# Last row tile of an attention and dense layer: its final product cut into 384 and 128 columns in place of 256 and 256

## The chip, the core and the metric

The kernel runs on one core of a Trainium2 chip. The metric is the time of one execution on the device in microseconds (us); three runs of the kernel before took 237.77, 237.84 and 237.99 us, median 237.84 us. TensorE multiplies matrices, VectorE (DVE) and ScalarE (ACT) work elementwise, GpSimd (POOL) does elementwise work and issues some transfers, and SyncE (SP) issues most transfers between device memory and on-chip memory.

## The reference, cut to what matters

The input `x` is 2048 rows of 512 columns. Each row is normalized, and two branches are added to it:

```python
xn  = layernorm(x)
q   = xn @ Wq.T + bq                      # only one head in four is used: 8 heads of 128
s   = elu(q) + 1
num = s @ M                               # per head, 128 x 128
den = s . z + 1e-6
att = repeat(num / den, 4) @ Wo.T         # back to 512 columns
ffn = xn @ (w.astype(float32) * w_scale) + b
out = x + att + ffn                       # 2048 x 512, float32
```

## The kernel before, in words

The 2048 rows are 16 tiles of 128 rows, called t = 0 to 15 (`T` = 16). The weights `Wo` are first summed over the four repeats and multiplied with `M` into one matrix `P` per head (8 heads, `G` = 8, each 128 x 512), so that the attention branch of a tile is one product: sum over the 8 heads of (128 rows x 128) by (128 x 512).

Every float32 product is made in three passes over operands split in two parts, a rounded high part and the rest, both in the format `F32R`. The function `three_passes` (L875 to L878) issues them: high by high (L876), then L877 and L878 with one low part each. In the rows of the trace the operand named `P_hi` or `P_lo` is the one that streams through TensorE (its columns set the width of the instruction), and `aT_hi` or `aT_lo` is the one loaded ahead into the array as weights, 128 x 128, by an instruction LDWEIGHTS (engine PEld in the trace).

TensorE is given its work in a written order: a start-up part, then for t = 7 to 15 the two q products, the dense product and the attention product of the tile eight before (`LAG` = 8), then the attention products of the remaining tiles 8 to 14 (`product_attn`, L951), and at last tile 15 (L1059 to L1068). A short transpose of the row means, `spread_mean` (L886), stands between the products in the loop.

Tile 15 differs from the others. Its 512 output columns are made in two pieces, c = 0 and c = 1, of 256 columns each, into two accumulators in different banks: `attn_ps[1]` and `q_ps[0]` (`last_attn_ps`, L106). For each piece TensorE runs over all 8 heads with three passes, 24 matmuls, and announces the piece on the semaphore `attn_filled`. VectorE waits for it and adds the accumulator onto the piece of `x` (L866 to L871, the instruction of L870), then announces `attn_added`. SyncE waits for that and issues the write of the piece to device memory (L300 to L303, the transfer of L303), and at the end waits for all writes (L304). While TensorE works on the second piece, the first is added and written.

The waits of TensorE for tile 15 stand only in the first piece: for the operands of tile 15 (`aT_lo_ready`) and for the accumulator to be free (`attn_added`).

Of the kernel before, what the change touches and what calls it, by code (L numbers as in the profile page):

```python
# [18 lines left out]
def retrieval_and_dense(nc, x_d, xT_d, x_pair_d, xT_pair_d, WqT_d, bq_d, WoT_d, MT_d, z_d, w_d, wscale_d, b_d, out_d):  # L19


    P = 128
    T, _, HID = x_d.shape
    _, G, D = MT_d.shape
    R, K, _, E = WqT_d.shape
    HALF = E // 2
    GH = G // 2
# [12 lines left out]
    with ExitStack() as ctx:  # L40
# [3 lines left out]
        def bank(name):  # L44
            return ctx.enter_context(nc.psum_tensor(name, [P, 512], F32))
# [50 lines left out]
        q_ps = [bank(f"q{i}_ps") for i in range(4)]  # L96
        dense_ps = bank("dense_ps")
        attn_ps = [bank("attn0_ps"), bank("attn1_ps")]
        mean_ps = bank("mean_ps")

        def q_bank(t, h):
            if t < LEAD and t % 3 == 1:
                return attn_ps[h]
            return q_ps[2 * (t % 3 == 2 if t < LEAD else t % 2) + h]

        def last_attn_ps(c):  # L106
            return [attn_ps[(T - 1) % 2], q_ps[0]][c][:, 0:HID // 2]

        x_in = [sem(f"x_in{t}") for t in range(T)]
        xT_in = [sem(f"xT_in{t}") for t in range(T)]  # L110
# [59 lines left out]
        def halves(h):  # L170
            return slice(h * HALF, (h + 1) * HALF)
# [13 lines left out]
        def place(t):  # L185
            return {T - 6: 2, T - 5: 3, T - 2: 2, T - 1: 3}.get(t, int(t >= 2 and t % 2 == 0))

        def aT_place(t):
            return [aT[:],
                    MT[:].rearrange("p g d -> p (g d)").rearrange("p (i e) -> p i e", i=4),  # L190
                    xT[:, 0:2].rearrange("p t k r -> p (t k r)").rearrange("p (i e) -> p i e", i=4),
                    xT[:, 2:4].rearrange("p t k r -> p (t k r)").rearrange("p (i e) -> p i e", i=4)][place(t)]

        def place_free(t):
            if t in (T - 6, T - 5):
                return xT_lo_ready, t + 5 + (t == T - 5)
            return aT_lo_ready, 2 * t - (6 if t >= T - 4 else 2)
# [13 lines left out]
        def groups_by_sync(t):  # L211
            return 4 if t < FIRST_SHARED else 3 if t == FIRST_SHARED else 2
# [4 lines left out]
        @block.sync  # L217
        def _(sp):
            def load_x(t):
                sp.dma_start(x[:, t, :], x_d[t]).then_inc(x_in[t], 16)  # L220

            def load_xT(t):
                if t >= XRING:
                    sp.wait_ge(xT_lo_ready, t - XRING + 2)
                sp.dma_start(xT[:, t % XRING, :, :].rearrange("p k r -> p (k r)"), xT_d[t]).then_inc(xT_in[t], 16)

            def load_wq_half(k, h):
                sp.dma_start(WqT_raw[:, k, halves(h)], WqT_d[0, k][:, halves(h)]).then_inc(wq_half_in[2 * k + h], 16)

            def load_wo(j):  # L230
                sp.dma_start(Wo_sum[:, j * GJ:(j + 1) * GJ, :].rearrange("p g c -> p (g c)"), WoT_d[0, j]
                             ).then_inc(wo_in[j], 16)

            def spread_blocks(t):
                sp.wait_ge(a_turned, t + 1)
                if t == 1:
                    sp.wait_ge(aT_lo_ready, 2)
                elif t == 2:
                    sp.wait_ge(P_filled, G)
                elif t >= 3:  # L240
                    sp.wait_ge(*place_free(t))
                for i in range(groups_by_sync(t)):
                    for j in range(4):
                        sp.dma_start(aT_place(t)[j * 32:(j + 1) * 32, i, :],
                                     sbuf_s[i * 32:(i + 1) * 32, t % SRING, j * E // 4:(j + 1) * E // 4]
                                     ).then_inc(aT_in[place(t)], 16)

            def store(t):
                sp.wait_ge(attn_added, t + 1)
                sp.dma_start(out_d[t], x[:, t, :]).then_inc(stored, 16)  # L250

            load_xT(0)
            load_wq_half(0, 1)
            load_wq_half(1, 0)
            load_wq_half(1, 1)
            load_wq_half(2, 0)
            load_wq_half(2, 1)
            load_wq_half(3, 0)
            load_wq_half(3, 1)
            load_x(2)  # L260
            load_xT(2)
            load_x(0)
            load_x(1)
            sp.dma_start(w_words, w_d).then_inc(w_in, 16)
            sp.dma_start(wd_raw, wscale_d).then_inc(wscale_in, 16)
            load_x(3)
            load_xT(3)
            sp.dma_start(bq_b[:], bq_d.unsqueeze(0).to_broadcast([P, E])).then_inc(bq_in, 16)
            load_wo(0)
            load_x(4)  # L270
            load_xT(4)
            load_wo(1)
            load_x(5)
            load_xT(5)
            sp.dma_start(z_b[:], z_d.unsqueeze(0).to_broadcast([P, E])).then_inc(z_in, 16)
            sp.dma_start(x[:, 6:8, :].rearrange("p t n -> p (t n)"), x_pair_d).then_inc(x_in[6], 16)
            sp.wait_ge(xT_lo_ready, 7 - XRING + 2)
            sp.dma_start(xT[:, 2:4, :, :].rearrange("p t k r -> p (t k r)"), xT_pair_d).then_inc(xT_in[6], 16)
            sp.dma_start(MT[:], MT_d).then_inc(M_in, 16)
            spread_blocks(0)  # L280
            for t in range(FIRST_LENT, LEAD + 4):
                sp.wait_ge(P_filled, t - FIRST_LENT + 1)
                load_x(t)
                load_xT(t)
            spread_blocks(1)
            for t in range(LEAD, T):
                if t + 4 < T:
                    sp.wait_ge(P_filled, t + 4 - FIRST_LENT + 1)
                    load_x(t + 4)
                    load_xT(t + 4)  # L290
                spread_blocks(t - BEHIND - 2)
                if t - LAG >= 1:
                    store(t - LAG - 1)
            for t in range(T - BEHIND - 2, T):
                spread_blocks(t)
                if T - BEHIND - 2 < t < T - 2:
                    store(t - BEHIND - 2)
            for t in range(T - 2 * BEHIND - 1, T - 1):
                store(t)
            for c in range(2):  # L300
                cols = slice(c * HID // 2, (c + 1) * HID // 2)
                sp.wait_ge(attn_added, T + c)
                sp.dma_start(out_d[T - 1][:, cols], x[:, T - 1, cols]).then_inc(stored, 16)  # L303
            sp.wait_ge(stored, 16 * (T + 1))  # L304
# [301 lines left out]
        def _(dve):  # L606
# [257 lines left out]
                    turn_blocks(T - 1)  # L864
                add_attn(t)
            for c in range(2):  # L866
                cols = slice(c * HID // 2, (c + 1) * HID // 2)
                dve.wait_ge(attn_filled, T + c)
                dve.wait_ge(b_added[T - 1], 16)
                nc.vector.tensor_tensor(x[:, T - 1, cols], last_attn_ps(c), x[:, T - 1, cols], ALU.add  # L870
                                        ).then_inc(attn_added, 1)  # L871

        @block.tensor
        def _(pe):
            def three_passes(out, x_hi, x_lo, w_hi, w_lo, start, stop):  # L875
                nc.tensor.matmul(out, x_hi, w_hi, start=start, stop=False)  # L876
                nc.tensor.matmul(out, x_hi, w_lo, start=False, stop=False)  # L877
                return nc.tensor.matmul(out, x_lo, w_hi, start=False, stop=stop)  # L878
# [178 lines left out]
            for t in range(T - LAG, T - 1):  # L1057
                product_attn(t)
            for c in range(2):  # L1059
                cols = slice(c * HID // 2, (c + 1) * HID // 2)  # L1060
                for g in range(G):
                    if c == 0 and g % GH == 0:
                        pe.wait_ge(aT_lo_ready, 2 * (T - 1) + g // GH + 1)
                    if c == 0 and g == 0:
                        pe.wait_ge(attn_added, T - 2)
                    last = three_passes(last_attn_ps(c), aT_hi[:, (T - 1) % 2, g, :], aT_lo[:, (T - 1) % 2, g, :],
                                        P_hi[:, g, cols], P_lo[:, g, cols], g == 0, g == G - 1)
                last.then_inc(attn_filled, 1)  # L1068
# [35 lines left out]
```

## Time and profile before

| what | value |
|---|---|
| median of three runs | 237.84 us |
| the profiled execution, its own time | 237.95 us |
| span in the profile, first to last instruction | 236.1 us |
| TensorE matmuls busy | 232.5 us, 98% of the span, 1037 instructions |
| weight loads (PEld) busy | 188.4 us, 80% |
| VectorE busy | 174.0 us, 74% |
| ScalarE busy | 125.2 us, 53% |
| GpSimd busy | 107.4 us, 45% |
| mean granted TensorE clock | 1.000 |

The span runs from the first to the last instruction; the time of the execution is 1.85 us more. Matmuls are pipelined: the trace draws each one longer than the distance to the next, so the pace of TensorE is read from the starts of successive instructions and not from their durations. Weight loads run beside the matmuls on a row of their own. "Landing" of a transfer is the time from its issue until its data has arrived.

### The profile page before, as it was taken

The numbers are of one execution on the slowest core, as the hardware profiler recorded it, in microseconds if no ns is written. First come the engines' busy times: TensorE is split into PE (matmuls) and PEld (weight loads), VectorE is DVE, ScalarE is ACT, GpSimd is POOL, SyncE is SP. The second block draws the span as 40 slices with busy tenths as digits, with TensorE's granted clock in tenths as the row PEclk, the third lists the DMA queues.
The fourth block names the chain that finished last, engine by engine and source line by source line (L and its number), as shares of the span: only waits on it lengthen the run. The fifth ranks groups of instructions, "written<-read, shape, count | busy, mean of one in ns | idle before, by whom it ended". The sixth has DMA issues, their size and how long they took to land.

```text
span 236.1 us, 3421 instructions
## 1 busy us (share of the span) xinstructions
PE 232.5 (98%) x1037; PEld 188.4 (80%) x1037; DVE 174.0 (74%) x275; ACT 125.2 (53%) x285; POOL 107.4 (45%) x117
## 2 busy tenths in 40 slices
PE   8999999999999999999999999999999999999995
PEld 3688788888888788888888888888888888888895
DVE  2989999897589987997858859585667879362511
ACT  4845358687298386585547253654637445630300
POOL 1029437856932356558350442524045598480000
PEclk9999999999999999999999999999999999999999
DMA  6999999999590144471727272431134456879521
GB/s 227 389 412 414 356 250 254 224 212 218 133 278 17 41 95 130 96 180 48 175 89 178 72 196 77 91 104 39 52 94 97 136 135 159 191 189 182 193 98 44
DMA packets 24081, 38.76 MB, mean 164 GB/s; under 512 B 5440, under 2 KB 13248, under 8 KB 22912
## 3 DMA queue, kind: packets, MB, share of 16 engines
q1 hardware_dynamic: 18816, 26.10, 33.7%
q0 software_dynamic: 3808, 11.14, 24.5%
q10 hardware_dynamic: 1440, 1.31, 1.9%
q8 instruction: 8, 0.13, 0.2%
q14 instruction: 9, 0.07, 0.1%
HBM read 25.95 MB, written 4.19 MB: 128 GB/s over the span
## 4 chain that ended last, share of the span: by engine, by line
PE 98%; DVE 0%; issue 0%
PE attn_ps L876 14%; PE attn_ps L878 14%; PE attn_ps L877 13%; PE q_ps L876 10%; PE q_ps L878 10%; PE q_ps L877 10%; PE dense_ps L876 6%; PE dense_ps L878 6%; PE dense_ps L877 6%; PE dense_ps L967 2%; PE q_ps L916 1%; PE q_ps L904 1%; PE q_ps L911 1%; PE attn_ps L916 1%; PE attn_ps L904 1%; PE attn_ps L911 1%
## 5 line engine op out<-in xcount | busy, mean ns | idle before, releaser
L489 ACT ACTIVATE s<-s,rden 128x128 f32<-128x128 f32 x128 | 39.2, 390 | 39.3 <-DVE rden L707 37.6
L341 POOL TENSOR_TENSOR e_and_sz<-s,z_b 128x512 f32<-128x512 f32 x32 | 41.7, 1340 | 39.6 <-DVE den L703 39.6
L876 PE MATMUL attn_ps<-P_hi,aT_hi 128*128 128x512 f32 (+1 forms) x136 | 53.0, 389 | 0.0
L878 PE MATMUL attn_ps<-P_hi,aT_lo 128*128 128x512 f32 (+1 forms) x136 | 52.2, 384 | 0.0
L877 PE MATMUL attn_ps<-P_lo,aT_hi 128*128 128x512 f32 (+1 forms) x136 | 52.1, 383 | 0.0
L876 PE MATMUL q_ps<-WqT_hi,xT_hi 128*128 128x512 f32 x104 | 40.7, 391 | 0.0
L878 PE MATMUL q_ps<-WqT_hi,xT_lo 128*128 128x512 f32 x104 | 40.5, 389 | 0.0
L877 PE MATMUL q_ps<-WqT_lo,xT_hi 128*128 128x512 f32 x104 | 40.5, 389 | 0.0
L691 DVE SCALAR_TENSOR_TENSOR q_ps<-q_ps,rstd,bq_b 128x512 f32<-128x512 f32 x28 | 21.0, 752 | 17.6 <-PE q_ps L878 17.6
L876 PEld LDWEIGHTS attn_ps<-P_hi,aT_hi 128*128 128x128 f32 x136 | 25.6, 188 | 6.1 <-issue 0.6
L878 PEld LDWEIGHTS attn_ps<-P_hi,aT_lo 128*128 128x128 f32 x136 | 25.6, 188 | 5.2
L877 PEld LDWEIGHTS attn_ps<-P_lo,aT_hi 128*128 128x128 f32 x136 | 25.6, 188 | 4.7
L316 POOL TENSOR_TENSOR xT<-xT,mean_b 128x512 f32<-128x512 f32 x13 | 18.9, 1454 | 22.9 <-ACT mean_b L430 22.9
L468 ACT ACTIVATE e_and_sz<-q_ps 128x512 f32<-128x512 f32 x28 | 16.6, 594 | 18.1 <-DVE q_ps L691 17.7
L876 PE MATMUL dense_ps<-wd_hi,xT_hi 128*128 128x512 f32 x64 | 25.3, 395 | 0.0
L878 PE MATMUL dense_ps<-wd_hi,xT_lo 128*128 128x512 f32 x64 | 25.0, 390 | 0.0
L877 PE MATMUL dense_ps<-wd_lo,xT_hi 128*128 128x512 f32 x64 | 24.9, 389 | 0.0
L716 DVE STREAM_TRANSPOSE s<-s 128x1024 f32<-128x1024 f32 x16 | 19.7, 1229 | 4.6 <-ACT s L489 4.6
L876 PEld LDWEIGHTS q_ps<-WqT_hi,xT_hi 128*128 128x128 f32 x104 | 19.5, 188 | 4.4 <-DVE xT_lo L650 0.3
L703 DVE TENSOR_REDUCE den<-e_and_sz 128x8 f32<-128x1032 f32 x16 | 19.4, 1214 | 4.8 <-POOL e_and_sz L341 4.8
L878 PEld LDWEIGHTS q_ps<-WqT_hi,xT_lo 128*128 128x128 f32 x104 | 19.5, 188 | 4.1
L877 PEld LDWEIGHTS q_ps<-WqT_lo,xT_hi 128*128 128x128 f32 x104 | 19.5, 188 | 4.0
(96 smaller groups left out, 356.1 us busy)
## 6 DMA issues: line engine op xcount, KB each, us to landing
x<-in_WoT POOLq DMA_DIRECT2D x6, 1024.0 KB, 11.0
x<-in_b POOLq DMA_DIRECT2D x16, 256.0 KB, 4.4
out<-x SPq DMA_DIRECT2D x15, 256.0 KB, 2.4
x<-in_x SPq DMA_DIRECT2D x14, 256.0 KB, 3.6
xT<-in_xT SPq DMA_DIRECT2D x13, 256.0 KB, 3.8
aT<-s SPq DMA_DIRECT2D x104, 32.0 KB, 2.3
MT<-s SPq DMA_DIRECT2D x72, 32.0 KB, 1.9
x<-in_WoT SPq DMA_DIRECT2D x2, 1024.0 KB, 13.3
```

Of the source, the lines that this page charges most:

```text
L316: nc.gpsimd.tensor_tensor(xT[:, t % XRING, :, :], xT[:, t % XRING, :, :], mean_b[:, t % 2, :].unsqueeze(1).to_broadcast([P, K, P]), ALU.su ...
L341: nc.gpsimd.tensor_tensor(sz_eps[:, :, h * D // 2:(h + 1) * D // 2].rearrange("p g (j c) -> p j g c", j=2), by_quarter(sbuf_s[:, t % SRING ...
L468: nc.scalar.activation(e, q_bank(t, h)[:], ACT.Relu, scale=-1.0).then_inc(qneg_ready, 1)
L489: last = nc.scalar.activation(a_g, a_g, ACT.Copy, scale=rden[:, t % 2, g:g + 1])
L691: nc.vector.scalar_tensor_tensor(q_bank(t, h)[:], q_bank(t, h)[:], rstd[:, t:t + 1], bq_b[:, halves(h)], ALU.mult, ALU.add).then_inc(q_bia ...
L703: nc.vector.reduce_sum(den[:, t % 2, :], sz_eps, AX.X).then_inc(den_ready, 1)
L716: nc.vector.transpose(sbuf_s[:, t % SRING, :], sbuf_s[:, t % SRING, :]).then_inc(a_turned, 1)
L876: nc.tensor.matmul(out, x_hi, w_hi, start=start, stop=False)
L877: nc.tensor.matmul(out, x_hi, w_lo, start=False, stop=False)
L878: return nc.tensor.matmul(out, x_lo, w_hi, start=False, stop=stop)
L904: nc.tensor.matmul(q_bank(t, h)[:], xT_hi[:, t, k, :], WqT_hi[:, k, halves(h)], start=k == 0, stop=False)
L911: nc.tensor.matmul(q_bank(t, h)[:], xT_lo[:, t, k, :], WqT_hi[:, k, halves(h)], start=False, stop=False)
```

## The change

The two pieces of tile 15 become 384 columns (`HID - P`) and 128 columns (`P`). The number of instructions, their order, the accumulators, the semaphores and their counts stay. The new helper `last_columns` gives the columns of a piece to SyncE, VectorE and TensorE.

```diff
+        def last_columns(c):
+            return [slice(0, HID - P), slice(HID - P, HID)][c]
+
         def last_attn_ps(c):
-            return [attn_ps[(T - 1) % 2], q_ps[0]][c][:, 0:HID // 2]
+            return [attn_ps[(T - 1) % 2], q_ps[0]][c][:, 0:[HID - P, P][c]]
...
             for c in range(2):
-                cols = slice(c * HID // 2, (c + 1) * HID // 2)
+                cols = last_columns(c)
                 sp.wait_ge(attn_added, T + c)
                 sp.dma_start(out_d[T - 1][:, cols], x[:, T - 1, cols]).then_inc(stored, 16)
...
             for c in range(2):
-                cols = slice(c * HID // 2, (c + 1) * HID // 2)
+                cols = last_columns(c)
                 dve.wait_ge(attn_filled, T + c)
                 dve.wait_ge(b_added[T - 1], 16)
                 nc.vector.tensor_tensor(x[:, T - 1, cols], last_attn_ps(c), x[:, T - 1, cols], ALU.add
...
             for c in range(2):
-                cols = slice(c * HID // 2, (c + 1) * HID // 2)
+                cols = last_columns(c)
                 for g in range(G):
```

The changed program has three more lines ahead of these places, so L876 of the kernel before is L879 of the changed one. On TensorE, at the seam between the two pieces (`attn1_ps` holds the first, `q0_ps` the second), the rows before are:

```order
L876 MATMUL attn1_ps<-P_hi,aT_hi 128x256
L877 MATMUL attn1_ps<-P_lo,aT_hi 128x256
L878 MATMUL attn1_ps<-P_hi,aT_lo 128x256
L876 MATMUL q0_ps<-P_hi,aT_hi 128x256
L877 MATMUL q0_ps<-P_lo,aT_hi 128x256
L878 MATMUL q0_ps<-P_hi,aT_lo 128x256
```

and in the changed kernel:

```order
L879 MATMUL attn1_ps<-P_hi,aT_hi 128x384
L880 MATMUL attn1_ps<-P_lo,aT_hi 128x384
L881 MATMUL attn1_ps<-P_hi,aT_lo 128x384
L879 MATMUL q0_ps<-P_hi,aT_hi 128x128
L880 MATMUL q0_ps<-P_lo,aT_hi 128x128
L881 MATMUL q0_ps<-P_hi,aT_lo 128x128
```

The sequence is the same; 24 rows in front of the seam grow to 384 columns, and 24 behind it shrink to 128. At the end of VectorE's program stand, before:

```order
L731 TENSOR_TENSOR x<-attn0_ps,x 128x512 [waits b_added12,attn_filled]
L724 TENSOR_TENSOR aT_lo<-xT,aT_hi 128x512 [waits attn_filled,aT_hi_ready] x2
L731 TENSOR_TENSOR x<-attn1_ps,x 128x512 [waits b_added13,attn_filled]
L724 TENSOR_TENSOR aT_lo<-xT,aT_hi 128x512 [waits attn_filled,aT_hi_ready] x2
L731 TENSOR_TENSOR x<-attn0_ps,x 128x512 [waits b_added14,attn_filled]
```

and in the changed kernel:

```order
L734 TENSOR_TENSOR x<-attn0_ps,x 128x512 [waits b_added12,attn_filled]
L727 TENSOR_TENSOR aT_lo<-xT,aT_hi 128x512 [waits attn_filled,aT_hi_ready] x2
L734 TENSOR_TENSOR x<-attn1_ps,x 128x512 [waits b_added13,attn_filled]
L727 TENSOR_TENSOR aT_lo<-xT,aT_hi 128x512 [waits attn_filled,aT_hi_ready] x2
L734 TENSOR_TENSOR x<-attn0_ps,x 128x512 [waits b_added14,attn_filled]
```

Only the widths of the last two additions differ. At the end of SyncE's program the two writes of tile 15 stand behind the same transfers as before; before:

```order
L244 DMA xT<-s 32x256 [waits aT_lo_ready,a_turned]
L244 DMA xT<-s 32x256 x7
L250 DMA out<-x 128x512 [waits attn_added] x6
L303 DMA out<-x 128x256 [waits attn_added] x2
L40 UNCONDITIONAL_BRANCH [waits stored]
```

and in the changed kernel:

```order
L247 DMA xT<-s 32x256 [waits aT_lo_ready,a_turned]
L247 DMA xT<-s 32x256 x7
L253 DMA out<-x 128x512 [waits attn_added] x6
L306 DMA out<-x 128x384 [waits attn_added]
L306 DMA out<-x 128x128 [waits attn_added]
L40 UNCONDITIONAL_BRANCH [waits stored]
```

They were two writes of 128 columns by two, and are now one of 384 columns and one of 128.

## Rows read from the trace of the kernel before

**Rows 1.** The page: slices of the span, granted clock, chain of waits.
```profile
PE   8999999999999999999999999999999999999995
PEclk9999999999999999999999999999999999999999
...
PE 98%; DVE 0%; issue 0%
```

**Rows 2.** TensorE in order of time, 216 us on: start us, us, instruction.
```profile
216.71 0.39 PE L876 MATMUL attn_ps<-P_hi,aT_hi 128*128 128x512 f32 x1
...
222.15 0.39 PE L876 MATMUL attn_ps<-P_hi,aT_hi 128*128 128x512 f32 x1
...
227.59 0.28 PE L876 MATMUL attn_ps<-P_hi,aT_hi 128*128 128x256 f32 x1
...
230.47 0.28 PE L876 MATMUL q_ps<-P_hi,aT_hi 128*128 128x256 f32 x1
...
233.22 0.28 PE L878 MATMUL q_ps<-P_hi,aT_lo 128*128 128x256 f32 x1
```

**Rows 3.** The end of the chain of waits: start us, us, what.
```profile
233.39 0.13 PE q_ps L878
233.52 0.02 issue
233.54 0.42 DVE x L870
```

**Rows 4.** Who waited for whom at the end: us in total, times, longest us.
```profile
DVE x L870 <- PE q_ps L878: 2.5, 1, 2.5
...
SPq L303 <- DVE x L870: 4.8, 2, 2.5
```

**Rows 5.** Groups by shape on TensorE and its weight loads: count, busy us, mean ns.
```profile
L876 PE MATMUL attn_ps<-P_hi,aT_hi 128*128 128x512 f32 x128 | 50.7, 396 | 0.0
...
L878 PE MATMUL q_ps<-P_hi,aT_lo 128*128 128x256 f32 x8 | 2.3, 282 | 0.0
...
L878 PEld LDWEIGHTS q_ps<-P_hi,aT_lo 128*128 128x128 f32 x8 | 1.5, 192 | 0.0
```

**Rows 6.** Weight loads beside the mean's transpose: start us, us, instruction.
```profile
142.93 0.27 PE L886 MATMUL mean_ps<-ident,meanvar 128*128 128x128 f32 x1
142.93 0.19 PEld L876 LDWEIGHTS attn_ps<-P_hi,aT_hi 128*128 128x128 f32 x1
...
143.04 0.19 PEld L877 LDWEIGHTS attn_ps<-P_lo,aT_hi 128*128 128x128 f32 x1
...
143.27 0.19 PEld L878 LDWEIGHTS attn_ps<-P_hi,aT_lo 128*128 128x128 f32 x1
```

**Rows 7.** Four weight loads in a row at 7.6 us, around a plain float32 product.
```profile
7.56 0.19 PEld L892 LDWEIGHTS q_ps<-aT 128*128 128x128 f32 x1 [0.23 <-DVE aT L625]
...
7.67 0.19 PEld L892 LDWEIGHTS q_ps<-aT 128*128 128x128 f32 x1
7.78 0.19 PEld L904 LDWEIGHTS q_ps<-WqT_hi,xT_hi 128*128 128x128 f32 x1
7.89 0.19 PEld L911 LDWEIGHTS q_ps<-WqT_hi,xT_lo 128*128 128x128 f32 x1
```

**Rows 8.** Groups by shape on VectorE: count, busy us, mean ns.
```profile
L731 DVE TENSOR_TENSOR x<-attn_ps,x 128x512 f32<-128x512 f32 x15 | 10.2, 677 | 12.2 <-PE attn_ps L878 11.9 <-issue 0.2
...
L625 DVE TENSOR_TENSOR aT<-mean_b 128x128 f32<-128x128 f32 x2 | 0.6, 292 | 0.1
...
L870 DVE TENSOR_TENSOR x<-q_ps,x 128x256 f32<-128x256 f32 x1 | 0.4, 424 | 2.5 <-PE q_ps L878 2.5
```

**Rows 9.** The transfers: issue of L303, landing of L250's writes and of groups.
```profile
L303 SPq DMA_DIRECT2D out<-x x2: 332/332/332, 231.1 to 234.0; - x2
...
DMA to landing us min/median/max: 2.0/2.4/4.0
...
MT<-s SPq DMA_DIRECT2D x72, 32.0 KB, 1.9
...
out<-x SPq DMA_DIRECT2D x2, 128.0 KB, 1.7
```

**Rows 10.** Bandwidth from 233.9 to 237 us in 40 equal slices.
```profile
GB/s 0 0 0 0 0 0 0 0 0 0 0 13 238 344 357 317 304 106 13 0 0 0 0 0 0 0 0 0 0 0 0 0 0 0 0 0 0 0 0 0
```

## The prediction

> **What bounds the kernel now.** I read the page first. TensorE is busy in every slice of the span and at the full granted clock, the level of 2.4 GHz, and the chain of waits that ended last is 98% TensorE [rows 1]. So the reader should look for one thing: how long TensorE's stream is, and what hangs behind its last matmul. For the stream I read the list in order of time. Of the last full tiles, 24 matmuls of 512 columns run from 216.71 to 222.15 us, so one takes a slot of 5.44 / 24 = 0.2267 us. In tile 15 the first piece runs from 227.59 to 230.47, 24 matmuls of 256 columns, 0.1200 us each; the second from 230.47 to the start of its last at 233.22, 23 slots of 0.1196 us [rows 2]. No waits stand between them. The end of the chain shows what is behind the stream: the last matmul ends, VectorE adds for 0.42 us from 233.54, SyncE issues the write at 234.0, and it lands 1.7 us later [rows 3, 9]. The waits say the same from the other side: VectorE stood for 2.5 us for the second piece, and SyncE 4.8 us in two waits for VectorE [rows 4]. Both are starved, TensorE is not. The first piece's addition and write lie under the second piece.
>
> **What a slot is made of.** From 256 to 512 columns a slot grows by 0.2267 - 0.1198 = 0.1069 us, or 0.418 ns a column, one column per cycle at 2.4 GHz. What is left beside the columns is 0.1198 - 0.1069 = 0.013 us. By columns alone, a slot of 384 is 0.1198 + 0.0534 = 0.1733 us and one of 128 is 0.1198 - 0.0534 = 0.066 us. The two would add up to the two of 256, and cutting at another column would cost TensorE nothing. But each matmul also needs its own weight load of 128 x 128, drawn 192 ns long [rows 5]. The number of loads doesn't shrink with the columns. How close can loads follow each other? Nowhere in the trace does an `F32R` matmul of 128 columns stand, so I look for places where short matmuls make the loads the limit. There are two. At 142.93 us a transpose of 128 columns starts together with the load for the product behind it, and the next load starts at 143.04, which in this stream is when that product starts: 0.11 us for a slot of 128 columns with a full load beside it, where the product of 512 columns behind it takes 0.23 again [rows 6]. At 7.56 us four loads start at 7.56, 7.67, 7.78 and 7.89: 0.110 us apart, the last two of them in `F32R` [rows 7]. Loads overlap each other and the matmuls, but they don't come closer than that in these rows. In the stream of 256 columns the load's 0.11 is just covered by the slot of 0.12. With 128 columns it isn't.
>
> **The change part by part.**
> First piece: 24 slots of 0.1733 = 4.16 us in place of 2.88, which is +1.28 us. It is an interpolation between two measured widths, good to about 0.05 us in all. All of it is on the path, since TensorE has no gap there.
> Second piece: 24 slots. Bounds are 0.110 us, the pitch of loads alone, which gives 2.64, and 0.120, if the 13 ns that every slot carries come on top, which gives 2.88. I take 0.115, between the two rows that speak for it: 2.76 us in place of 24 x 0.1196 = 2.87, so -0.11 (bounds -0.23 and 0.00). The wider bounds, in which something other than load pitch decides, are the rivals below: 0.066 and 0.22.
> Last matmul: from start to end it is drawn 389 to 396 ns at 512 columns and 283 at 256 [rows 5], so 53 ns shorter at 128: -0.05.
> Last addition: 424 ns at 256 columns. A two-operand addition of 128 x 128 took 292 ns [rows 8], and the slope of 677 at 512 to 424 at 256 gives about the same. -0.13.
> Last write: its issue is 0.33 us whatever the size. A piece of 128 KB landed after 1.7 us, of which the bandwidth row shows data moving for some 7 slices of 0.078 us, 0.5 us. Halving the data can save at most half of that, 0.25. The writes of 256 KB landed after 2.0 at best, 0.3 more for twice the data, which gives 0.15. On the other side, transfers of only 32 KB in short pieces took 1.9, which is 0.2 more than 1.7 [rows 9, 10]. I take -0.12, nearest to the rows of the same kind of write, and keep -0.25 and +0.2 as ends.
> First addition and write: they grow, and they are hidden. The first piece's last matmul starts at 227.59 + 23 x 0.1733 = 231.58 and ends at 231.91; the addition of 384 columns takes 0.42 + 0.13 = 0.56, so the write is issued at about 232.56 and is down at 234.6 even if it takes the 2.0 us of a full tile. The second piece is added only at 234.96 by my slots and its write issued at 235.0. Cover: 0.4 us. If it were gone, the last write would share the channels with the end of the first, and wait behind it for what is missing.
> Nothing ahead of 227.59 is touched: the operands of tile 15 and the free accumulator are there before TensorE asks, as the gapless start of the piece shows. The waits are the same, and nothing is moved past another queue.
> Sum: +1.28 - 0.11 - 0.05 - 0.13 - 0.12 = +0.87 us. Against the profiled execution's own 237.95 us (the span of 236.1 and 1.85 around it) this is 238.82; against the median of the runs, 237.84, which is 0.11 lower, 238.71. I give the latter, 238.7. With the bounds (0.05 on the first piece, 0.12 on the second, 0.13 and 0.32 on the write, 0.05 on the small terms) it goes from +0.5 to +1.4: 238.4 to 239.2.
>
> The load's price is the term on which the sign rests, and a page speaks against mine. The rows show loads 0.110 us apart and 0.11 us for the slot of the transpose [rows 6, 7]. The Trainium skill, "TensorE: Matmul & The Clock Gate", section "Back-to-back issue gap", says that a stream of pairs of load and matmul sustains about 81 ns per matmul at 128 columns. By it the second piece would take 24 x 0.081 = 1.94 us, and the sum would be +0.05. The same sentence gives 131 ns at 512 columns, where this trace has 227 [rows 2], so its operands are evidently lighter ones, and I let the rows decide.
>
> **The rivals.**
> A, not slower: loads are hidden entirely. If the loads can run further ahead than one, so that the columns set the slot, it is 0.066 us, the second piece takes 24 x 0.066 = 1.59 and gives back 1.28. TensorE's stream is then as long as before and only the shorter tail is left: -0.30, which is 237.5. For it: the slot fits one column per cycle exactly at 256 and 512, and four loads at 7.6 us overlap each other. Against: in the same rows they keep 0.11 apart, and in tile 15 load and matmul start at the same moment throughout. It decides as soon as the pitch of loads can fall under about 0.079 us, where the sum crosses zero. The rule of the Trainium skill that I named would end here too.
> B, narrow `F32R` matmuls lose their pace and go as plain float32 does. A plain float32 product of 128 columns stands in the trace as two loads and two matmuls, and takes from 7.56 to 7.78, 0.22 us [rows 7]. That is also what 512 columns take. Then the second piece is 24 x 0.22 = 5.28, +2.41, and the sum +3.4: 241.2. For it: no `F32R` matmul under 256 columns stands in this trace, so nothing shows that the pace holds there. Against: nothing shows either that the width changes the way the operands are read, and between 512 and 256 it is straight.
> C, the load is not hidden under a short matmul but comes behind its columns: 0.11 + 0.053 = 0.163 us a slot, 3.92 for the piece, +1.05: the sum is +2.0, 239.9. Against it is the transpose's slot of 0.11, though a transpose may be read otherwise than a product.
>
> **How the numbers follow.** My forecast 0.72, with its own range of 238.4 to 239.2; rival A (and what lies between it and me) 0.10; B 0.13; C 0.05. The range of 8 in 10 is 237.8 to 240.0: it takes in C and the upper part of A, and leaves out B and the rest of A, together some 0.18. What a measurement of this kernel can tell from no change is 0.2%, 0.48 us, so no change is 237.36 to 238.32. My forecast, B and C are slower, less a little for a forecast that falls short: 0.88. A is no change, 0.09, and faster only if the write saves its most besides, 0.03.
>
> **What would show it.** In the changed profile the 24 matmuls of 384 columns should start 0.173 apart and the second piece at 231.75; its matmuls of 128 columns 0.110 to 0.120 apart with weight loads that start back to back at that same distance, and the last one should start at about 234.4. The addition should be 0.29 us, its write issued about 235.0 and down about 1.6 later, with the first piece's write down before that. A distance of 0.07 to 0.08 in the second piece shows A, 0.16 C, 0.2 or more B. If the first piece's slots differ from 0.173, or if the last write takes longer than 1.7, the sum is wrong in that term; if the distance is under 0.08, the sign is.

## The result, and the profile after

The changed kernel is slower by a third of a per cent: 238.82 us median (238.48 to 238.96, 7 runs) against 237.96 (237.77 to 238.13, 7 runs), ratio 1.0034 with a 95% interval of 1.0024 to 1.0044, or +0.86 us. The span of the profiled execution went from 236.1 to 237.0 us.

The two writes of tile 15 were of 256 columns each before the change. The two additions of VectorE whose widths differ are these in the traces (start us, us, instruction), before:

```profile
230.67 0.42 DVE L870 TENSOR_TENSOR x<-attn_ps,x 128x256 f32<-128x256 f32 x1 [2.18 <-PE attn_ps L878]
233.54 0.42 DVE L870 TENSOR_TENSOR x<-q_ps,x 128x256 f32<-128x256 f32 x1 [2.45 <-PE q_ps L878]
```

and after:

```profile
232.12 0.56 DVE L873 TENSOR_TENSOR x<-attn_ps,x 128x384 f32<-128x384 f32 x1 [3.49 <-PE attn_ps L881]
234.75 0.29 DVE L873 TENSOR_TENSOR x<-q_ps,x 128x128 f32<-128x128 f32 x1 [2.07 <-PE q_ps L881]
```

The page of the changed kernel answers to [rows 1]: busy time of the engines, and the clock in 40 slices.

```profile
PE 233.3 (98%) x1037; PEld 189.5 (80%) x1037; DVE 174.3 (74%) x275; ACT 125.0 (53%) x285; POOL 107.5 (45%) x117
...
PEclk9999999999999999999999999999999999999999
```

The number of instructions is the same and so is the clock; TensorE is 0.8 us longer busy. Where, the list in order of time shows (start us, us, instruction), at the ends of the two pieces, to be laid beside [rows 2]:

```profile
227.74 0.33 PE L879 MATMUL attn_ps<-P_hi,aT_hi 128*128 128x384 f32 x1
...
231.58 0.33 PE L880 MATMUL attn_ps<-P_lo,aT_hi 128*128 128x384 f32 x1
231.58 0.19 PEld L881 LDWEIGHTS attn_ps<-P_hi,aT_lo 128*128 128x128 f32 x1
231.75 0.33 PE L881 MATMUL attn_ps<-P_hi,aT_lo 128*128 128x384 f32 x1
231.75 0.19 PEld L879 LDWEIGHTS q_ps<-P_hi,aT_hi 128*128 128x128 f32 x1
231.92 0.22 PE L879 MATMUL q_ps<-P_hi,aT_hi 128*128 128x128 f32 x1
231.93 0.19 PEld L880 LDWEIGHTS q_ps<-P_lo,aT_hi 128*128 128x128 f32 x1
231.98 0.27 PE L880 MATMUL q_ps<-P_lo,aT_hi 128*128 128x128 f32 x1
232.03 0.19 PEld L881 LDWEIGHTS q_ps<-P_hi,aT_lo 128*128 128x128 f32 x1
...
234.38 0.19 PEld L881 LDWEIGHTS q_ps<-P_hi,aT_lo 128*128 128x128 f32 x1
234.44 0.28 PE L881 MATMUL q_ps<-P_hi,aT_lo 128*128 128x128 f32 x1
234.75 0.29 DVE L873 TENSOR_TENSOR x<-q_ps,x 128x128 f32<-128x128 f32 x1 [2.07 <-PE q_ps L881]
```

Three things are to be seen. In the wide piece each load starts with the matmul before its own, and 24 slots take 4.18 us, 0.174 each. In the narrow piece the loads run back to back: 22 distances from 231.93 to 234.38, 2.45 us, 0.1114 each (the matmuls, from 231.98 to 234.44, 0.1118 each), where the columns with the 13 ns beside them would ask for 0.066. And the drawn length of a narrow matmul tells it too: the first is 0.22 us long, all later ones 0.27 to 0.28, since they are drawn from when the array takes them up, 0.06 us behind their load, and stand there until that load is through. So the 0.06 us between the first two drawn starts is not the first slot: the second matmul's load began only at 231.93, with the first matmul, and the weights were there about 0.11 later.

The chain of waits, in order of time (start us, us, what), shows the same at the seam, beside [rows 3]:

```profile
231.91 0.17 PE attn_ps L881
232.08 0.06 PE q_ps L879
232.14 0.11 PE q_ps L880
232.26 0.11 PE q_ps L881
...
234.60 0.13 PE q_ps L881
234.73 0.02 issue
234.75 0.29 DVE x L873
```

The first narrow matmul ends 0.06 us behind the last wide one, since its weights were loaded under that one (from 231.75); each of the 23 behind it ends 0.11 after the one before.

SyncE's issues of the two writes of tile 15 and the time until they land, beside [rows 9]:

```profile
L306 SPq DMA_DIRECT2D out<-x x2: 332/332/332, 232.7 to 235.1; - x2
...
DMA to landing us min/median/max: 1.6/1.7/1.9
```

From its first start to its last end TensorE needs 6.98 us for tile 15 (227.74 to 234.72) in place of 5.91 (227.59 to 233.50): +1.07. From that end to the end of the span there are 2.28 us in place of 2.60: -0.32. That makes +0.75 for the last tile. In the profiled execution tile 15 also begins 0.15 us later, with nothing changed ahead of it; in the eight experiments below that start lies anywhere between 227.55 and 228.53, so single profiles are compared from it on. What moves it is open.

### The profile page after: what moved, and what is told of

Its sections match the earlier page's. It is cut to its first block, busy times and chain, and to the rows that moved or that the text cites. A ratio compares the mean times of both kernels' runs of the same rounds, so it can differ in the third digit from the quotient of the medians.

```text
span 237.0 us, 3421 instructions
## 1 busy us (share of the span) xinstructions
PE 233.3 (98%) x1037; PEld 189.5 (80%) x1037; DVE 174.3 (74%) x275; ACT 125.0 (53%) x285; POOL 107.5 (45%) x117
## 4 chain that ended last, share of the span: by engine, by line
PE 88%; DVE 4%; DMA 3%; SPq 2%; issue 2%; ACT 1%
PE attn_ps L879 14%; PE attn_ps L881 14%; PE attn_ps L880 14%; PE q_ps L879 10%; PE q_ps L881 10%; PE q_ps L880 10%; PE dense_ps L879 6%; PE dense_ps L881 6%; PE dense_ps L880 6%; DMA aT<-in_w 3%; SPq L231 1%; DVE wd_lo L671 1%; DVE q_ps L694 1%; SPq L223 1%; PE mean_ps L889 1%
## 5 line engine op out<-in xcount | busy, mean ns | idle before, releaser
L879 PE MATMUL attn_ps<-P_hi,aT_hi 128*128 128x512 f32 (+1 forms) x136 | 53.4, 392 | 0.0
L879 PE MATMUL q_ps<-WqT_hi,xT_hi 128*128 128x512 f32 x104 | 40.7, 391 | 0.1
L879 PEld LDWEIGHTS attn_ps<-P_hi,aT_hi 128*128 128x128 f32 x136 | 25.5, 188 | 6.1 <-issue 0.6
L879 PE MATMUL dense_ps<-wd_hi,xT_hi 128*128 128x512 f32 x64 | 25.3, 395 | 0.0
L879 PEld LDWEIGHTS q_ps<-WqT_hi,xT_hi 128*128 128x128 f32 x104 | 19.5, 188 | 4.5 <-DVE xT_lo L653 0.5
```

## The experiments

Theory L: the weight load of the next matmul sets the slot when it takes longer than the columns. Rival N: a narrow `F32R` matmul is slow by itself, at two cycles a column, whatever it loads. Eight kernels tell them apart and price the terms. A slot in the table is the mean distance of the matmuls' starts, from the second one of the piece on. All times are medians; "last tile" is from TensorE's first start in tile 15 to its last end, "tail" from there to the end of the span, both of the profiled execution.

| kernel | second piece, slot us | last tile us | tail us | sum against before | measured against before |
|---|---|---|---|---|---|
| before, 256 and 256 | 0.120 | 5.91 | 2.60 | | |
| changed, 384 and 128 | 0.112 | 6.98 | 2.28 | +0.75 | +0.86 |
| e1, 384 and 128, half the weights | 0.060 | 5.78 | 2.29 | -0.44 | -0.45 |
| e2, 320 and 192 | 0.112 | 6.34 | 2.44 | +0.27 | +0.28 |
| e3, 448 and 64 | 0.111 | 7.63 | 2.16 | +1.28 | +1.28 |
| e4, 384 and 128 alternating | 0.286 a pair | 6.98 | 3.09 | +1.56 | +1.45 |
| e5, 128 then 384 | 0.174 (first piece 0.11) | 7.04 | 2.89 | +1.42 | +1.33 |
| e6, 512 undivided | 0.227 | 5.61 | 3.17 | +0.27 | +0.24 |
| e7, 272 and 240 | 0.112 | 5.86 | 2.61 | -0.04 | -0.12 |
| e8, 256 and 256, half the weights | 0.114 | 5.77 | 2.58 | -0.16 | -0.11 |

**e1: half the weights.** The weights of the second piece are cut to 64 columns:

```diff
-three_passes(last_attn_ps(c), aT_hi[:, (T - 1) % 2, g, :], aT_lo[:, (T - 1) % 2, g, :],
+three_passes(last_attn_ps(c)[0:[P, P // 2][c], :], aT_hi[:, (T - 1) % 2, g, 0:[P, P // 2][c]],
+             aT_lo[:, (T - 1) % 2, g, 0:[P, P // 2][c]],
```

> The second piece (128 columns) is made for the first 64 rows of the tile only, so each of its 24 weight loads brings 64 columns of weights in place of 128; the number of matmuls and their 128 streamed columns stay. The lower 64 rows of that piece are left out. Theory L (the next matmul's weight load sets the slot, 0.111 us for 128 columns of weights): the load falls to about 0.055, the columns set the slot again, 0.066 us; the piece takes 24 x 0.066 = 1.6 us in place of 2.7, total about 238.82 - 1.07 = 237.75. Rival N (a narrow F32R matmul is itself slow, whatever it loads): slots stay at 0.111, total 238.8.

Measured 237.53 us (237.35 to 238.82, 10 runs) beside 237.98 for the kernel before, ratio 0.9983 (0.9962 to 1.0003): not clear of the kernel before, but some 1.3 us under the changed one, where N expected no difference from it. The narrow piece, in order of time:

```profile
233.97 0.22 PE L879 MATMUL q_ps<-P_hi,aT_hi 128*64 128x128 f32 x1
233.97 0.14 PEld L880 LDWEIGHTS q_ps<-P_lo,aT_hi 128*64 128x64 f32 x1
234.03 0.22 PE L880 MATMUL q_ps<-P_lo,aT_hi 128*64 128x128 f32 x1
234.03 0.14 PEld L881 LDWEIGHTS q_ps<-P_hi,aT_lo 128*64 128x64 f32 x1
234.09 0.22 PE L881 MATMUL q_ps<-P_hi,aT_lo 128*64 128x128 f32 x1
```

The same 24 matmuls with the same 128 streamed columns now follow at 0.060 us, and are drawn 0.22 long, without the wait. The columns that stream through have not changed, so N is out. The edit halves two things, though: a load brings 64 columns of weights, and each matmul writes 64 rows of the accumulator. It can't tell a load that takes 0.111 us from a floor of 0.111 us that a matmul writing 128 rows would have by itself; the rows of e3 can. That the slot fell to 0.060 and not to 0.066 is taken up by e8.

**e2: 320 and 192 columns.** Here and in e3, e5 and e7 only the widths in `last_columns` and `last_attn_ps` change:

```diff
-            return [slice(0, HID - P), slice(HID - P, HID)][c]
+            return [slice(0, 320), slice(320, HID)][c]
...
-            return [attn_ps[(T - 1) % 2], q_ps[0]][c][:, 0:[HID - P, P][c]]
+            return [attn_ps[(T - 1) % 2], q_ps[0]][c][:, 0:[320, HID - 320][c]]
```

> Pieces of 320 and 192 columns. Theory L: first piece 24 x 0.1465 = 3.52 us, second 24 x 0.111 = 2.67 (its columns alone would be 0.093), sum 6.19 against 5.75 with 256 and 256, +0.44; last addition 0.36 in place of 0.42, last write about 0.09 shorter: total about 237.96 + 0.29 = 238.25. Rival N, at two cycles a column below 256 (0.107 measured at 128 is 256 cycles): 192 columns take 0.160 to 0.173, second piece 3.8 to 4.2, total 239.3 to 239.7.

(The 0.107 called measured there is 256 cycles at 2.4 GHz; the trace of the changed kernel has 0.1114 to 0.1118.)

Measured 238.26 us (237.95 to 238.94, 10 runs), ratio 1.0009 (0.9991 to 1.0026): the total alone is not clear of no change, but it excludes N's 239.3, and the trace decides. Matmuls and loads at the end of the narrow piece, in order of time:

```profile
233.84 0.27 PE L881 MATMUL q_ps<-P_hi,aT_lo 128*128 128x192 f32 x1
233.86 0.19 PEld L879 LDWEIGHTS q_ps<-P_hi,aT_hi 128*128 128x128 f32 x1
233.95 0.27 PE L879 MATMUL q_ps<-P_hi,aT_hi 128*128 128x192 f32 x1
233.97 0.19 PEld L880 LDWEIGHTS q_ps<-P_lo,aT_hi 128*128 128x128 f32 x1
234.06 0.28 PE L880 MATMUL q_ps<-P_lo,aT_hi 128*128 128x192 f32 x1
```

With 192 columns the distance is the same 0.11 as with 128. The total came out as expected, 238.26 for 238.25.

**e3: 448 and 64 columns.**

> Pieces of 448 and 64 columns. Theory L: first piece 24 x 0.200 = 4.80, second again 24 x 0.111 = 2.67 though it has half the columns, sum 7.47, +1.72; last addition 0.225 in place of 0.42 and the last write shorter by 0.2: total about 237.96 + 1.3 = 239.3. Rival N, two cycles a column: 64 columns take 0.053 to 0.067, second piece 1.3 to 1.6, sum +0.4 to +0.65, total 238.0 to 238.3.

Measured 239.26 us (239.02 to 239.5, 10 runs), ratio 1.0045 (1.003 to 1.0061). In order of time, the last matmuls:

```profile
235.04 0.28 PE L879 MATMUL q_ps<-P_hi,aT_hi 128*128 128x64 f32 x1
235.12 0.19 PEld L880 LDWEIGHTS q_ps<-P_lo,aT_hi 128*128 128x128 f32 x1
235.15 0.28 PE L880 MATMUL q_ps<-P_lo,aT_hi 128*128 128x64 f32 x1
235.23 0.19 PEld L881 LDWEIGHTS q_ps<-P_hi,aT_lo 128*128 128x128 f32 x1
235.26 0.28 PE L881 MATMUL q_ps<-P_hi,aT_lo 128*128 128x64 f32 x1
```

Half the columns of the changed kernel, and the same 0.11. At 64, 128 and 192 columns the slot is flat.

The starts also say whose the floor is. In the wide pieces a load starts together with the matmul ahead of its own (231.58 and 231.75 in the changed kernel). If it does so here too, its start tells when that matmul begins to stream. The matmul that the load is for is drawn 0.03 us behind it here (235.12 and 235.15), 0.06 in the changed kernel and 0.09 in e2: what 64, 128 and 192 columns alone take at 0.418 ns each (0.027, 0.053 and 0.080). So the matmul ahead hands on after its own columns, however narrow it is, and the rest of the 0.11 us the next one stands and waits, drawn 0.28 long. A floor of the matmul itself would leave no such short distance. This is an argument from the starts in the traces; no run changes the load without changing the rows written.

A miss by little: the wide slots of 448 columns took 4.87 / 24 = 0.203 and not 0.200; why is open.

**e4: wide and narrow alternating.** The passes are issued as pairs, with the same waits; `pass_of(0, ...)` issues one pass of the wide piece, `pass_of(1, ...)` one of the narrow. `BEHIND_WIDE` is 0, so the second condition always holds (cut to the loop):

```diff
+            for i, (g, p) in enumerate(passes):
+                pass_of(0, g, p)
+                if i >= BEHIND_WIDE:
+                    pass_of(1, *passes[i - BEHIND_WIDE])
```

> Same 384 and 128 columns, but each narrow matmul stands right behind a wide one (wide, narrow, wide, narrow) and not in one block. Both pieces end together, so the tail is longer (both additions behind the last matmul: about +0.6 us). Theory L with one load ahead (a load may begin only when the matmul before its own begins): behind each narrow matmul the wide one's load of 0.111 is still exposed, pair 0.173 + 0.111 = 0.284, 24 pairs 6.8 us as in the block; total about 238.82 + 0.6 = 239.4. Theory L with loads queued freely: two loads of 0.111 fit under a pair's columns of 0.240, 24 pairs 5.75 us; total about 238.4. Rival N gives 0.284 as well; it is told apart by the half weights.

Measured 239.43 us (239.22 to 241.01, 10 runs), ratio 1.0061 (1.004 to 1.0083). A narrow matmul, the wide one behind it and the next narrow one, in order of time:

```profile
233.92 0.22 PE L1070 MATMUL q_ps<-P_hi,aT_hi 128*128 128x128 f32 x1
233.92 0.19 PEld L1070 LDWEIGHTS attn_ps<-P_lo,aT_hi 128*128 128x128 f32 x1
233.97 0.39 PE L1070 MATMUL attn_ps<-P_lo,aT_hi 128*128 128x384 f32 x1
234.03 0.19 PEld L1070 LDWEIGHTS q_ps<-P_lo,aT_hi 128*128 128x128 f32 x1
234.20 0.22 PE L1070 MATMUL q_ps<-P_lo,aT_hi 128*128 128x128 f32 x1
234.21 0.19 PEld L1070 LDWEIGHTS attn_ps<-P_hi,aT_lo 128*128 128x128 f32 x1
```

A pair takes 0.286 us (23 distances of the narrow ones from 227.90 to 234.49, 0.2865), as in the block (0.174 + 0.112), and the last tile the same 6.98. The tail is 0.81 longer than in the changed kernel, where 0.6 was expected, since both additions and both writes now stand at the end of the stream. Now it is the wide matmul that is drawn longer, 0.39 in place of 0.33: it stands behind a narrow one and waits for its own load, which began only at 233.92. The load of the next narrow one begins at 234.03, when the wide one has its weights. So one load runs ahead and no more: spare time under a wide matmul can't be saved up, and a slot is the longer of a matmul's own columns and the load of the one behind it. That is what [rows 6] showed beside the transpose.

**e5: the narrow piece first.**

> The narrow piece first: 128 columns, then 384. TensorE has the same 48 matmuls in two blocks, so theory L expects the same stream as in the changed kernel: 24 x 0.111 + 23 x 0.173 + 0.336 = 6.99 us from the first start to the last end (6.98 there). The tail is the one of the wide piece: addition 0.56 in place of 0.29 and a write of 192 KB in place of 64, about 0.3 longer. Total about 238.82 + 0.57 = 239.4. A rival in which the changed kernel's tail saved nothing (its small write as slow as a large one) expects only the addition's 0.27: 239.1.

Measured 239.28 us (239.09 to 239.4, 6 runs), ratio 1.0047 (1.0032 to 1.0061), and 7.04 us for the last tile. The total lies between the two that were expected, 239.4 and 239.1, and its interval holds both, so the trace has to decide. The stream pays for the narrow piece wherever it stands; the tail is 0.61 longer than in the changed kernel, which prices what the narrow end saves: 0.27 in the addition and the rest in a write that landed after 1.9 us in place of 1.6.

**e6: tile 15 undivided.** `range(2)` becomes `range(1)` in the three loops, with one write.

> Tile 15 in one piece of 512 columns: 24 matmuls of 0.2267, from first start to last end 23 x 0.2267 + 0.39 = 5.60 us against 5.91 with 256 and 256: -0.31, since half of the 13 ns per matmul go. One addition of 0.69 in place of 0.42 and one write of 256 KB, 2.0 to 2.3 in place of 1.7, stand behind it: +0.27 + 0.3. Total about 237.96 + 0.26 = 238.2.

Measured 238.19 us (238.1 to 238.93, 12 runs), ratio 1.0011 (1.0000 to 1.0021). The last tile takes 5.61 and the tail 3.17. Dividing in halves costs the stream 0.30 us and gives 0.57 in the tail.

**e7: 272 and 240 columns.**

> Pieces of 272 and 240 columns, just above the width at which the load takes over (0.1114 - 0.013 = 0.098 us, 236 columns). Theory L: second piece's slots 0.1131 by columns, 24 x (0.1265 + 0.1131) = 5.75 as with 256 and 256; the tail is 0.02 to 0.03 shorter. Total 237.93, no difference that can be measured. A threshold at 256 columns, whatever its cause, would show as slots other than 0.113.

Measured 237.83 us (237.54 to 238.47, 12 runs), ratio 0.9989 (0.9979 to 0.9999). It has the lowest median of those that do all the work, 0.12 us under the kernel before, at the edge of what can be told from nothing; stream and tail of its trace account for 0.04. That it is faster is not shown. The end of the narrow piece, in order of time:

```profile
233.29 0.27 PE L879 MATMUL q_ps<-P_hi,aT_hi 128*128 128x240 f32 x1
233.29 0.19 PEld L880 LDWEIGHTS q_ps<-P_lo,aT_hi 128*128 128x128 f32 x1
233.40 0.27 PE L880 MATMUL q_ps<-P_lo,aT_hi 128*128 128x240 f32 x1
233.40 0.19 PEld L881 LDWEIGHTS q_ps<-P_hi,aT_lo 128*128 128x128 f32 x1
```

22 slots from 231.05 to 233.51 give 0.112 us, where the columns with their 13 ns gave 0.113. There is no step at 256 columns: 240 lie where the line of the columns meets the floor of the load.

**e8: 256 and 256 columns with half the weights.** The edit of e1 in the kernel before.

> The kernel before (256 and 256 columns), the second piece made for the first 64 rows only, so that its weight loads bring 64 columns. The other 64 rows of that piece are left out. It asks where the 13 ns beside the columns come from, since with half weights a slot of 128 columns was 0.060 and not 0.066. If they belong to the weights (half the weights, half of it), the slots are 0.1067 + 0.0066 = 0.113 and the total about 0.15 less, 237.8; if they belong to the matmul, the slots stay at 0.1197 and the total at 237.96.

Measured 237.84 us (237.57 to 240.2, 12 runs), ratio 0.9999 (0.998 to 1.0017): the total can't decide 0.15 us. The end of the second piece, in order of time:

```profile
232.82 0.13 PEld L877 LDWEIGHTS q_ps<-P_lo,aT_hi 128*64 128x64 f32 x1
232.93 0.28 PE L877 MATMUL q_ps<-P_lo,aT_hi 128*64 128x256 f32 x1
232.93 0.13 PEld L878 LDWEIGHTS q_ps<-P_hi,aT_lo 128*64 128x64 f32 x1
233.04 0.28 PE L878 MATMUL q_ps<-P_hi,aT_lo 128*64 128x256 f32 x1
```

The slots can decide: 23 from 230.42 to 233.04 take 0.1139 us, while the first piece of the same run, with whole weights, took 24 slots from 227.55 to 230.42, 0.1196. So of the 13 ns beside 256 columns about 7 are left with half the weights, and of 128 columns likewise 0.060 - 0.053 = 0.007 in e1. What costs these 13 ns beside the columns shrinks with the weights, or with the rows written, which were halved with them; by what path is open.

## Why the prediction was right

It gave 238.7 us and a slowdown of 0.87; measured are 238.82 and 0.86. The mechanism is the one forecast, and the sign rests on it; that the number hit within 0.01 is luck. The interval of the slowdown runs from 0.57 to 1.05 us, and the terms as the one trace shows them add up to +0.75. By its steps:

1. **TensorE bounds, and nothing waits in tile 15.** Right: its stream has no gap but the loads, and the measured totals follow stream plus tail within 0.11 us in all nine kernels.
2. **First piece +1.28.** Measured 4.18 - 2.88 = +1.30.
3. **Second piece by the load's pitch.** The deciding step, right in kind: e1 removes the floor with the loads, e2 and e3 show it flat. I took 0.115 between 0.110 and 0.120; it was 0.1114 by the loads and 0.1118 by the matmuls. The 13 ns, which I had allowed to come on top, come on top of the columns alone. So 24 slots gave 24 x (0.1118 - 0.1196) = -0.19 in place of -0.11.
4. **Last matmul -0.05.** The list draws it 275 ns long and not 230, because it is drawn while it still waits for its load. Its load began at 234.38, so at a pitch of 0.11 its weights were there at about 234.49, and it ended 0.23 later: counted so, the -0.05 holds. Steps 3 and 4 together, from the first start of the second piece to its last end, were forecast at -0.16 and are 2.80 - 3.03 = -0.23; the stream as a whole was forecast at +1.12 and is +1.07.
5. **Last addition -0.13.** Measured 424 to 292 ns, -0.13.
6. **Last write -0.12.** It landed after 1.6 in place of 1.7. The tail as a whole fell by 0.32, 0.25 of it forecast; what is left beside the addition is 0.19 where 0.12 was forecast, with 0.05 of rounding on either span.
7. **The first write is hidden.** Right: issued at 232.7, landed after 1.9, down at 234.6, before the last one's issue at 235.1.

Rival A (loads hidden entirely) is refuted by the 0.111 to 0.112 of every narrow piece with whole weights. So is the 81 ns at 128 columns that I weighed from the Trainium skill, "TensorE: Matmul & The Clock Gate", section "Back-to-back issue gap". Its section "LDWEIGHTS (loading the stationary operand)" says that a load takes its column count over 1.2 GHz. For 128 columns that makes an estimate of 107 ns; the traces, with loads 0.1114 us apart, agree within 5 ns. Rival B (the pace of plain float32, 0.22) is refuted by the same slots; it was the rival with the highest chance, for want of any narrow `F32R` matmul in the trace before. Rival C (the load behind the matmul's own columns, 0.163) is refuted too: the columns of the narrow matmul lie wholly under the load.

## What to carry to other kernels

In a stream of matmuls that each bring new weights, price a slot as the longer of its own columns and the next one's weight load, here 0.111 us for 128 columns of `F32R` weights. Cutting an output unevenly to shorten the tail can pay only down to the width at which the two meet, here 236 to 240 columns (an estimate from the pitch of 0.1114, 13 ns and 0.418 ns a column, and the slot of e7); below it every column taken off the last piece is added to the other piece and takes nothing off its own slots. That any uneven cut pays is not shown: the best, 272 and 240, was at the edge of no difference. Wide matmuls in between don't help, since only one load runs ahead.

## What the runs showed of the hardware that was not expected

- The fixed part of a slot isn't a constant of the matmul: about 13 ns with weights of 128 columns, 7 ns with 64 (e1, e8).
- A waiting matmul is drawn longer, not later: 0.28 in place of 0.22 at 128 columns, 0.39 in place of 0.33 for the wide one behind a narrow one. "Idle before" stays at zero, so the stall shows only in lengths that don't fit the width.
- A write of one tile's rows with no other write just before it landed after 1.4 us at 32 KB (e3), 1.6 at 64, 1.7 at 128, 1.9 at 192 and 2.0 at 256 (e6): 0.3 us from 32 to 128 KB and again 0.3 from there to 256.
